# An early-fusion transformer layer on one core: the loop over groups of the attention stage written out on all engines

## What is computed

```python
h = tok(x)                                   # norm, project, norm, class token, positions
h = concatenate([h, txt], axis=1)            # (32, 69, 256)
h = h + attn(_layernorm(h))
h = h + ffn(_layernorm(h))

def attn(x):
    q = einsum('bsd,hpd->bhsp', x, q_w) + q_b        # k and v alike
    scores = einsum('bhqp,bhkp->bhqk', q, k) / sqrt(64)
    attn = softmax(scores, axis=2)
    ctx = einsum('bhqk,bhkp->bqhp', attn, v)
    return ctx.reshape(...) @ l_w.T + l_b

def ffn(x):                                  # top 2 of 8 experts, capacity, ranks by cumsum
    h = gelu(einsum('ecd,edf->ecf', exp_batches, c_fc))
    exp_out = einsum('ecf,efd->ecd', h, c_proj)
    return cb_weight @ exp_out
```

## Time and profile before

| | us |
|---|---|
| median of 3 runs | 806.3 |
| the profiled execution | 806.62 |
| its span, first to last instruction | 805.0 |
| PE busy with matmuls | 712.6 (89%) |
| DVE busy | 523.5 (65%) |
| ACT busy | 294.1 (37%) |
| POOL busy | 277.1 (34%) |
| instructions | 17117 |
| mean granted clock of PE | 0.922 |

### The profile page before, as it was taken

The page is one execution under the profiler, slowest core; times in us unless marked ns, Lnnn a source line. Parts: engine busy times, 40 slices in busy tenths (PEclk is TensorE's granted clock), DMA queues, the critical chain, the costliest instruction groups (busy, mean ns, idle before and its releaser), DMA issues.

```text
span 805.0 us, 17117 instructions
## 1 busy us (share of the span) xinstructions
PE 712.6 (89%) x6527; PEld 665.0 (83%) x6527; DVE 523.5 (65%) x1143; ACT 294.1 (37%) x652; POOL 277.1 (34%) x293
## 2 busy tenths in 40 slices
PE   5979999979979899799799675089999999999996
PEld 4869888868868788688789565089999999999995
DVE  4992668867857768668668773255747657476561
ACT  3545554524425334245254220142524325243240
POOL 3671001030030120300201213634666665666615
PEclk9998999999989899989799756579999999999998
DMA  8530000000000000000000102414443454434312
GB/s 268 178 104 17 1 2 5 13 16 16 2 16 16 3 16 16 16 16 2 16 16 2 30 1 80 146 44 117 100 83 79 95 138 92 88 82 90 78 14 27
DMA packets 51266, 43.02 MB, mean 53 GB/s; under 512 B 25383, under 2 KB 44757, under 8 KB 51201
## 3 DMA queue, kind: packets, MB, share of 16 engines
q1 hardware_dynamic: 21729, 30.20, 12.2%
q0 software_dynamic: 29472, 11.90, 9.3%
HBM read 32.76 MB, written 10.25 MB: 53 GB/s over the span
## 4 chain that ended last, share of the span: by engine, by line
PE 57%; issue 25%; DVE 6%; DMA 5%; POOL 3%; ACT 2%; POOLq 1%; SPq 0%; DVEq 0%; ACTq 0%
PE shared L1310 9%; PE shared L1311 8%; PE shared L1312 8%; PE pair L1312 7%; PE pair L1310 7%; PE pair L1311 7%; DMA token_rows<-sent 4%; PE pair L1425 2%; PE ct_ps L1435 2%; PE vt_ps L1412 2%; PE ct_ps L1334 1%; PE shared L1471 1%; PE ct_ps L1564 1%; PE pair L1320 1%; POOL prob L617 1%
## 5 line engine op out<-in xcount | busy, mean ns | idle before, releaser
L775 ACT ACTIVATE qkv<-shared,bq_sb 128x276 f32<-128x276 f32 x192 | 93.7, 488 | 128.3 <-PE shared L1312 125.1
L1310 PE MATMUL shared<-xT_hi,wq_hi 128*128 128x276 f32 x384 | 127.0, 331 | 4.2 <-ACT x2T L813 1.5
L713 POOL DMA_INDIRECT out<-yrow,held x48 | 100.9, 2101 | 74.3 <-DVE yrow L1272 60.2
L1311 PE MATMUL shared<-xT_lo,wq_hi 128*128 128x276 f32 x384 | 114.0, 297 | 0.0
L1312 PE MATMUL shared<-xT_hi,wq_lo 128*128 128x276 f32 x384 | 113.4, 295 | 0.0
L885 ACT ACTIVATE act_f<-pair 128x348 f32<-128x348 f32 (+1 forms) x128 | 51.8, 457 | 97.3 <-PE pair L1312 97.3
L1310 PEld LDWEIGHTS shared<-xT_hi,wq_hi 128*128 128x128 f32 x384 | 75.2, 196 | 12.6 <-ACT x2T L813 2.6
L1310 PE MATMUL pair<-xe_hi,fc_hi 128*128 128x348 f32 (+1 forms) x256 | 82.7, 323 | 1.1 <-DVE xe_lo L1254 1.1
L1312 PE MATMUL pair<-xe_hi,fc_lo 128*128 128x348 f32 (+1 forms) x256 | 83.0, 324 | 0.0
L1311 PE MATMUL pair<-xe_lo,fc_hi 128*128 128x348 f32 (+1 forms) x256 | 82.9, 324 | 0.0
L696 POOL DMA_INDIRECT held<-token_rows,found_ix x48 | 67.9, 1414 | 26.7 <-issue 19.6
(11 more groups left out here) (179 smaller groups left out, 1737.2 us busy)
## 6 DMA issues: line engine op xcount, KB each, us to landing
raw_fc<-c_fc SPq DMA_DIRECT2D x8, 1024.0 KB, 7.2
raw_pj<-c_proj SPq DMA_DIRECT2D x8, 1024.0 KB, 7.5
qkv<-w_qkv SPq DMA_DIRECT2D x6, 512.0 KB, 7.4
qkv<-patches SPq DMA_DIRECT2D x6, 384.0 KB, 4.8
token_rows<-sent POOLq DMA_DIRECT2D x8, 285.7 KB, 7.1
out<-h SPq DMA_DIRECT2D x8, 276.0 KB
more_patches<-patches SPq DMA_DIRECT2D x3, 384.0 KB, 9.0
qkv<-w_l SPq DMA_DIRECT2D x1, 1024.0 KB, 7.8
```

The source lines that it names most:

```text
L713: pool.indirect_dma_start(out, bass.IndirectOffsetOnAxis(ap=xg[p][0:n, t, D:D + 1].bitcast(U32), axis=0), yrow[p][0:n, t, :], None, bounds ...
L775: act.activation(qkv[(st.i + shift) % 2][:, c, :], shared[bank][:, 0:GT], ACT.Identity, bias=bq_sb[:, c:c + 1]).then_inc(s_free[bank], 1)
L1310: pe.matmul(dst, l_hi, r_hi, start=(first and n == 0), stop=False)
L1311: pe.matmul(dst, l_hi, r_lo, start=False, stop=False)
```

## The change

`sweep` gets a guard for an empty loop, and the attention stage's call on each of the five engines asks for all 8 passes as the head. The expert stage's calls stay as they are. No operation, tile, order or semaphore is changed; lines behind `sweep` move down by one.

```diff
@@ -133,9 +133,10 @@
     for i in range(head):
         body(Step(i))
-    with eng.Fori(0, (n - head - tail) // span) as k:
-        for i in range(head, head + span):
-            body(Step(i, k, span))
+    if n > head + tail:
+        with eng.Fori(0, (n - head - tail) // span) as k:
+            for i in range(head, head + span):
+                body(Step(i, k, span))
     for i in range(n - tail, n):
         body(Step(i))
...
-            sweep(sp, stage_b, GROUPS, 1, 3, 2)
+            sweep(sp, stage_b, GROUPS, GROUPS, 0, 2)
...
-            sweep(pool, stage_b, GROUPS, 2, 2, 2)
+            sweep(pool, stage_b, GROUPS, GROUPS, 0, 2)
...
-            sweep(act, stage_b, GROUPS, 2, 2, 2)
+            sweep(act, stage_b, GROUPS, GROUPS, 0, 2)
...
-            sweep(dve, stage_b, GROUPS, 2, 2, 2)
+            sweep(dve, stage_b, GROUPS, GROUPS, 0, 2)
...
-            sweep(pe, stage_b, GROUPS, 2, 2, 2)
+            sweep(pe, stage_b, GROUPS, GROUPS, 0, 2)
```

## The result

| | before | after |
|---|---|---|
| median of 8 runs each, side by side | 806.34 us (805.72 to 808.27) | 803.11 us (801.83 to 804.15) |
| ratio, 95% interval | 1 | 0.9954 (0.9943 to 0.9966) |
| the profiled execution | 806.62 us | 802.34 us |
| its span | 805.0 us | 800.6 us |
| mean granted clock of PE | 0.922 | 0.926 |

The change takes 3.2 us off the median where 0.3 were forecast. The time lies in the stated range, but it is faster by 0.46%, which is beyond the 0.3% that a measurement can tell from no change, and the likeliest case was "within".

A forecast was written before the change was run, and what follows sets the result against it. The attention stage was taken as a ring through POOL's tail and `xn`, with PE at a slow clock after each stall; -1.2 - 0.4 + 1.3 = -0.3 us gave a median of 806.0 us, range 802.0 to 808.5 us.

The forecast's parts named there:

- the likeliest case: Whole kernel: time stays within 803.9 to 808.7 us, not told from no change; chance 0.60.
- The sum's own lower end: Whole kernel: the forecast with its terms at their fast ends, 803.3 us.
- the first rival: Register address slows `xn`, or DVE now precedes POOL: `xn` falls to about 1.05 us, around 801.4 us; chance 0.10.
- The ring and its order: Attention stage: `e_gap`, POOL's tail, `n_rs`, `xn`, PE's transposes, PE's pass, `e_gap` again; period 54 to 55 us.
- Term 1: POOL's tail, `e_gap` to `xn`, without register instructions: 2.20 us shorter in all, counted as -1.2 us.
- only 0.55 of it is kept: PE's restart after the stall: stall plus slow-clock stretch stay near 12 to 13 us, so 0.55 of saved tail counts.
- Term 2: Register instructions on PE, DVE and ACT inside a pass: 0.1 us in each of four passes, -0.4 us.
- Term 3: PE's branch back: 2.67 us idle but covered, so worth nothing; without it pass 4 gets stall and slow clock, +1.3 us.
- `xn` stays at 2.54 us: DVE's `xn` in the loop: stays slow because POOL adds positions meanwhile; no gain, a possible 1.5 us a pass put at 0.
- late code fetch: PE, mid-pass: longer streamed code comes late once, costing 5.6 us, 811.6 us in all; slower rival, chance 0.06.
- The fourth rival: Pass 7 and the stage's end: PE's clock falls elsewhere; 3 us faster, chance 0.12, or 3 us slower, chance 0.07.
- A sign of being wrong: Profile after: fast `xn` beside POOL's additions, pass 4 without slow stretch, PE "issue" gap inside a pass, or pass 7's clock falling elsewhere.

## Why the prediction was off, step by step

- **The likeliest outcome: wrong; the range held with some luck.** The sum's own lower end was 803.3 us, just above the 803.11 measured. The range reached to 802.0 for the sake of the first rival, which did not occur, and of the clock, which gave 1.4 us in place of 3.
- **The ring and its order: right.** One wait bounds each pass, and shortening the way from `e_gap` to `xn` moved the time. What else moved it is the clock in the passes and behind them.
- **Term 1, the size of POOL's tail: too small.** The link behind pass 1, 7.26 us, was taken for that of any written-out pass. It is a little longer than the others for itself, 7.21 us even now, where they are 7.09 to 7.12; the four looped links lost 0.77, 0.69, 0.71 and 0.67, 2.84 us and not 2.20, and with the first boundary PE restarts 3.09 us earlier. The tail behind pass 1 is 0.1 us longer than the others at its DMA alone.
- **Term 1, "only 0.55 of it is kept": the step that failed.** It rested on stall plus slow stretch staying near 12 to 13 us. After the change they are 10.8, 11.6, 11.8, 12.5 and 9.3 us. In passes 3 and 5, where the stall lost 0.81 us, the slow stretch gained 0.3 and not 0.8; in passes 2 and 6 it became shorter, by 0.8 and 2.6 us. Passes 2, 3, 5 and 6 take 1.09 us less together, 1.01 of it in pass 6, where the clock was down for 6.8 us and not 10.2. That part is not shown to be the tail's doing, as pass 6 has 6.8 us with only PE written out and the old tail, too. Four rows with a nearly constant sum were no law: added tail was kept at 1.0 and 1.25 of its size, and equal stalls had unequal slow stretches. The term was -1.2 in the forecast, and measured -3.09 for the boundaries and -1.09 for the passes' clock.
- **Term 2, register instructions inside a pass, -0.4: not found.** By the prediction's own reckoning the remainders of passes 2, 3 and 5 were 41.55, 41.42, 41.42 and are now about 41.5, 41.4, 41.4. Only PE written out gained nothing in the median either (0.9997).
- **Term 3, the branch is covered, and pass 4 loses 1.3 us: right.** PE alone written out gave 0.9997. Pass 4 went from 43.12 to 44.49 us, +1.37, with a stall of 5.02 us and a slow stretch. The reason given also held: without the cover the same branch costs 5.3 us.
- **`xn` stays at 2.54 us: right,** and so was the reason, POOL's addition; the first rival's mechanism did not occur.
- **No late code fetch:** no gap of kind "issue" at the end of pass 3. The largest wait of that kind on PE, 5.5 us at L1498 in the waits view, is in both kernels.
- **The clock behind pass 6:** -1.43 us that no term had. Most of it goes with the last long slow stretch, which begins at 491 us and lasts 37.5 us after and 41.0 before. The fourth rival had its kind, at 3 us. The length goes with the edits, though why is not shown: 37.5 us in the six profiles that have POOL's short tail and the root in its old place, 41.0 in the eight with a longer tail or the root early, the fastest kernel among them. The other 0.38 us lies in pass 7: from `e_gap` of pass 6 to that of pass 7 it is 39.8 us in the four profiles in which DVE, ACT and SP loop, and 39.4 in the ten in which they don't.
- **A sign of being wrong did show:** the clock falls in pass 7 at 450 us and not at 454. Of these 4.5 us, 3.0 are the earlier `e_gap` of pass 6. The other signs did not.

By the trace: -3.09 - 1.09 + 1.37 - 0.16 - 1.43 = -4.40 us of span. The medians of the runs keep 3.2 of it.

## What to carry to other kernels

Find the one wait that closes a pass and trace it back: only instructions on that way pay, here some 0.7 us of POOL's register instructions a pass, while a 2.7-us branch on the busiest engine was free under the wait, and cost 5.3 us where no wait covered it. So put the order right first (one root ahead of a wait it doesn't need gave 25 us, the loops written out 3.2 before that and 9.3 after it), then unroll, since that is when the branch comes into the open. And do not discount a saved stall by a slow stretch that is assumed to grow in its place: here the slow stretches moved either way.

## What the hardware showed that was not expected

- With `add_positions` moved, 5.8 us less of stalls in the ring went with 13.6 us less at the low clock: 3.4 us in each of passes 4 to 6 instead of 6.8, 10.2 and 6.8, and 6.8 as before in passes 2 and 3. The ring lost 9.7 us.
- In the loop, with its address and semaphore values in registers, POOL's DMA began 0.92 us behind the operation ahead of it; written out, 0.39 us. That is most of what a looped pass cost.
- With the clock never down, the same 2627 matmuls of the ring count 228.1 us of busy time instead of 242.0.
